# Attention stage of a three-part block: four tiles at a time instead of two, weights moved between ScalarE, VectorE and TensorE

## What is computed

```python
h = x.shape[-1]
proj = x @ W_proj.T
delta, Bs, Cs, residual = jnp.split(proj, 4, axis=-1)
delta = jax.nn.softplus(delta @ W_delta.T + b_delta)
A1 = A[0, 0]
B1 = Bp[0, :, 0]
dA = jnp.exp(delta * A1) * B1
dB = jnp.cumsum(delta * B1, axis=1)
uC = jnp.sum(x * Cs, axis=1, keepdims=True)
Csum = jnp.sum(Cs, axis=1, keepdims=True)
y = dA * uC + dB * Csum
return y + residual * D
...
x = x + 0.5 * _L0_ffn_ref(_layernorm(x, axis=-1), ...)
x = x + _L0_attn_ref(_layernorm(x, axis=-1), ...)
x = x + 0.5 * _L0_ffn_ref(_layernorm(x, axis=-1), ...)
```

## Time and profile before

| | us |
|---|---|
| median of three runs | 1527.41 |
| lowest and highest | 1524.95, 1527.49 |
| the profiled execution, timed from outside | 1527.63 |
| its span, from the first to the last instruction | 1525.8 |
| first and last `x_new` of the attention stage begin at | 649.9, 1096.4 |
| five batches in a row, `a_sums` to `a_sums` | 57.0 each |

### The profile page before, as it was taken

How to read it: one execution, slowest core, us unless ns; L and a number is a source line. 1 busy time by engine, 2 the same in 40 slices (tenths; PEclk the granted TensorE clock), 3 DMA queues, 4 the chain that set the end, 5 groups by cost and what they waited for, 6 DMA issues and landing times. The chain is left out here.

```text
span 1525.8 us, 31260 instructions
## 1 busy us (share of the span) xinstructions
PE 1298.1 (85%) x10212; PEld 1229.3 (81%) x10215; DVE 1239.9 (81%) x3385; ACT 1088.4 (71%) x2343; POOL 675.9 (44%) x778
## 2 busy tenths in 40 slices
PE   5555029999999999799999999987639999999996
PEld 4334019999999999599888888986529999999996
DVE  8999408999999998388999999999837777777775
ACT  6778117777777775589889888886537777777773
POOL 0577752444334444222254554544633344434443
PEclk8877559999999999899999999999859999999999
DMA  9979546766667661921111232111144444444440
GB/s 325 346 271 378 198 160 206 234 223 227 232 207 234 218 212 61 291 72 35 36 62 53 73 102 84 47 60 53 54 144 128 125 148 129 145 147 130 148 130 25
DMA packets 149776, 234.74 MB, mean 154 GB/s; under 512 B 24333, under 2 KB 124390, under 8 KB 147568
## 3 DMA queue, kind: packets, MB, share of 16 engines
q1 hardware_dynamic: 121968, 188.24, 38.2%
q0 software_dynamic: 27648, 44.50, 8.5%
HBM read 128.51 MB, written 136.48 MB: 174 GB/s over the span
## 5 line engine op out<-in xcount | busy, mean ns | idle before, releaser
L1034 PE MATMUL ps<-xs,ws 128*128 128x320 f32 x3072 | 469.6, 311 | 2.2 <-issue 2.2
L1034 PEld LDWEIGHTS ps<-xs,ws 128*128 128x128 f32 x3072 | 454.7, 189 | 8.2 <-issue 8.2
L859 POOL DMA_INDIRECT slots_and_rows<-x x160 | 161.5, 1010 | 238.1 <-DVE x L976 198.5
L859 POOL DMA_INDIRECT out<-x x160 | 157.8, 987 | 236.5 <-DVE x L966 153.8
L1034 PE MATMUL ps<-ws,hs 128*128 128x256 f32 x1920 | 260.6, 289 | 1.3 <-DVE hs L955 1.3
L1034 PEld LDWEIGHTS ps<-ws,hs 128*128 128x128 f32 x1920 | 239.0, 190 | 1.7 <-DVE hs L955 1.7
L898 ACT ACTIVATE x<-x 128x256 f32<-128x256 f32 x320 | 165.0, 594 | 64.8 <-DMA x<-slots_and_rows 49.2
L880 ACT CAST xs<-ps 128x512 fp32r<-128x512 f32 (+1 forms) x192 | 98.3, 513 | 130.4 <-PE ps L1027 130.4
L987 DVE TENSOR_TENSOR hf<-ps,sg 128x320 f32<-128x320 f32 x256 | 124.6, 487 | 81.6 <-ACT sg L919 77.7
L948 DVE TENSOR_TENSOR xs<-ps,xs 128x512 fp32r<-128x512 f32 (+1 forms) x192 | 113.5, 592 | 72.5 <-ACT xs L880 72.5
L373 POOL DMA_INDIRECT slots<-x,slot x128 | 132.9, 1038 | 79.7 <-issue 43.7
(11 more groups left out here) (139 smaller groups left out, 2282.8 us busy)
## 6 DMA issues: line engine op xcount, KB each, us to landing
slots<-blank SPq DMA_DIRECT2D x16, 1310.0 KB
slots_and_rows<-blank SPq DMA_DIRECT2D x32, 655.0 KB, 4.8
x<-slots_and_rows SPq DMA_DIRECT2D x31, 655.0 KB, 3.9
x<-slots SPq DMA_DIRECT2D x31, 655.0 KB, 4.0
x<-slots_and_rows SPq DMA_DIRECT2D x32, 516.0 KB, 8.7
x<-in_x SPq DMA_DIRECT2D x32, 512.0 KB, 8.7
wraw<-in_w_gate SPq DMA_DIRECT2D x64, 256.0 KB
wraw<-in_w_up SPq DMA_DIRECT2D x64, 256.0 KB
```

The source lines that it names most:

```text
L859: nc.gpsimd.indirect_dma_start(out=rows, out_offset=bass.IndirectOffsetOnAxis(ap=factor(e, k, F_ID).bitcast(U32), axis=0), in_=XG[:, e % G ...
L1034: ins = pe.matmul(dst, left(a, k), right(b, k), start=(n == 0), stop=(n == len(terms) - 1))
```

## The change

Softplus, cumulative sum, exponential and mix are done for four tiles (two pairs, called a unit m, 512 rows) at a time. The two PSUM banks now hold one half h of a unit each.

- VectorE: softplus, scan and mix are 128x512 instead of 128x256, half as many. The scan runs in place over CS with a constant 1 as factor. Its two halves stand apart: half 0 in the odd step, behind softplus of the same unit; half 1 at the head of the next step, ahead of the mix. The mix multiplies the exponential by u.
- ScalarE: a new piece, `weight`, makes CS = v*AB + v*b (L1284 of the changed kernel, two instructions of 128x512), at the head of the odd step; `d_a` uses a plain bias. |z+b|, exp, ln and d_a are twice as wide. The logarithm of |u| goes.
- PE: y is turned back by four transposes for a pair, ahead of the residual's products, in place of eight passes against the sign matrices.
- `a_factors` loses the size, sign and diagonal instructions and gains one.
- Buffers: XS has 5 slots, not 3. A pair lies two steps longer in the pipeline (x_new in step n+5, not n+3), and all routing lags move by two steps.

The diff, cut:

```diff
-                TURN, DELTA, PLUS, RES, BACK, LOGIT = 0, 1, 2, 3, 4, 5
+                TURN, DELTA, PLUS, RES, NEW, BACK, LOGIT = 0, 1, 3, 4, 5, 5, 7
...
+                    def weight(m):
+                        a = 2 * m // NC
+                        act.wait_ge(factors.sem, factors.at(a + 1))
+                        act.wait_ge(softplus_done.sem, softplus_done.at(m + 1))
...
                         for h in range(HC):
-                            ins = act.activation(LB[:, a % 2, 1, h:h + 1], LB[:, a % 2, 0, h:h + 1], ACT.Identity,
-                                                 bias=ABD[:, h:h + 1])
-                        ins.then_inc(biased.sem, 1)
...
+                            ins = act.activation(CS[:, m % 2, h, :], AB[:, m % 2, h, :], ACT.Identity,
+                                                 bias=UV[:, a % 2, 2, h:h + 1], scale=UV[:, a % 2, 1, h:h + 1])
+                        ins.then_inc(weighted.sem, 1)
...
                         for h in range(HC):
-                            ins = act.activation(YT[:, n % 2, h, :], AB[:, n % 2, h, :], ACT.Exp,
-                                                 bias=LB[:, a % 2, 1, h:h + 1], scale=A1[:, h:h + 1])
+                            ins = act.activation(YT[:, m % 2, h, :], AB[:, m % 2, h, :], ACT.Exp,
+                                                 bias=ABD[:, h:h + 1], scale=A1[:, h:h + 1])
...
-                        dve.scalar_tensor_tensor(uv[:, 2, :], uv[:, 0, :], -1.0, uv[:, 0, :], ALU.mult, ALU.max)
-                        dve.tensor_scalar(uv[:, 5, :], uv[:, 0, :], 0.0, 2.0, ALU.is_ge, ALU.mult).then_inc(f_links.sem, 1)
...
-                        for h in range(HC):
-                            ins = dve.tensor_scalar(DIAG[:, a % 2, h, :], IDENT, uv[:, 6, h:h + 1], None, ALU.mult)
-                        ins.then_inc(diag.sem, 1)
-                        dve.wait_ge(f_links.sem, f_links.next())
+                        dve.tensor_tensor(uv[:, 2, :], uv[:, 1, :], BD, ALU.mult).then_inc(factors.sem, 1)
...
+                    def scan(m, h):
+                        dve.wait_ge(weighted.sem, weighted.at(m + 1))
+                        dve.wait_ge(scanned.sem, scanned.at(m))
+                        apart(dve)
+                        start = 0.0 if 2 * m % NC == 0 else CS[:, 1 - m % 2, h, QT - 1:QT]
+                        ins = dve.tensor_tensor_scan(CS[:, m % 2, h, :], ONE1[:].to_broadcast([P, QT]), CS[:, m % 2, h, :],
+                                                     start, ALU.mult, ALU.add)
...
-                                ins = pe.matmul(ps[:, BY, j * H + h * P:j * H + (h + 1) * P],
-                                                YT[:, n % 2, h, j * P:(j + 1) * P], DIAG[:, t % 2, h, :],
-                                                start=False, stop=(h == HC - 1), skip_group_check=True)
...
+                                pe.matmul(ps[:, BY, j * H + h * P:j * H + (h + 1) * P],
+                                          YT[:, n // 2 % 2, h, n % 2 * CT + j * P:n % 2 * CT + (j + 1) * P], IDENT,
+                                          start=(j + h == 0), stop=False,
+                                          is_transpose=True, skip_group_check=True)
```

More of the change, by code:

```diff
@@ L1076, in attention @@
                 BZ = (2, 6)
+                QT, XB = 2 * CT, 5
                 stream = stream2
@@ L1249, in x_hi @@
                         act.wait_ge(b_turned.sem, b_turned.at(n + 1))
[L1250 to L1256, removed]
+                        act.wait_ge(residual_done.sem, residual_done.at(n - XB + 1))
@@ L1295, in scalar @@
                         for n in soon(S, TURN):
                             x_hi(n)
+                        for n in at(S, BACK + 1):
+                            tail.act_evac(act, n)
+                        for m in unit(S, PLUS):
+                            d_a(m)
                         for c in parts(S, [p[1] + 1 for p in POST_AT]):
@@ L1420, in vector @@
                             a_sums(a)
-                        for n in soon(S, PLUS):
-                            softplus(n)
+                        for m in unit(S, PLUS + 1):
+                            scan(m, 1)
+                            mix(m)
+                        for n in at(S, NEW):
+                            x_new(n)
+                        for n in at(S, NEW):
+                            dve.wait_ge(x_added.sem, x_added.at(n + 1))
+                            apart(dve)
+                            tail.dve_stats(dve, n)
+                        for m in summed(S):
+                            softplus(m)
                         chosen(S, 5, True)
@@ L1444, in vector @@
                                     tail.dve_moments(dve, n // 2)
+                        for m in unit(S, PLUS):
+                            scan(m, 0)
                         for part in (3, 4, 5, 6, 1, 2, 0):
@@ L1538, in tensor @@
                             sums(a)
+                        for n in at(S, RES):
+                            if n % 2 == 1:
+                                residual(n)
                         for n in soon(S, DELTA):
@@ L1541, in tensor @@
                         counts(S, True)
+                        for n in at(S, RES):
+                            if n % 2 == 0:
+                                residual(n)
                         for n in at(S, LOGIT + 1):
```

173 lines of the change are left out of this document (76 added, 97 removed).

## The result

| | before | after |
|---|---|---|
| median of four runs, us | 1527.41 | 1551.92 |
| lowest and highest | 1524.95, 1527.49 | 1546.23, 1553.4 |
| ratio after to before, 95% interval | | 1.0165 [1.0143, 1.0187] |
| profiled execution, timed from outside | 1527.63 | 1551.43 |
| its span | 1525.8 | 1549.6 |

The change costs 24.5 us; 10.7 were forecast. The direction and the stall were as predicted, the size was not. After the last `x_new` nothing changed: 1525.8 - 1096.4 = 429.4 us remain before, 1549.6 - 1120.1 = 429.5 after.

The account below looks back on a forecast made before the run. VectorE was taken to set the step. Net 0.46 us in 31 double steps gave +14.3; with -6.6, -2.3, +5.0 and +0.3 the sum was +10.7 us, so 1538 us, range 1521 to 1553.

Parts of the forecast that it names:

- Start: Start of the attention stage, up to the first `x_new`: it would come 0.3 us later.
- VectorE, the new wait: VectorE before the scan's half 0: standing 1.68 us for `weight` in place of 0.04, 1.64 us lost a double step.
- ScalarE: ScalarE at 12.15 us a double step: later than VectorE by 0.50 without routing, in some 10 of 31, +5 us.
- PE: Four transposes replace eight sign-matrix passes: 0.3 us a pair saved but hidden; no bound of its own, costs or gives nothing.
- VectorE, width: Wider softplus, scan and mix on VectorE: 1.18 us saved in a double step, 1.05 to 1.30 with the ends.
- The end: Last unit's chain through softplus, weight, scans, mix and residuals, with routing pieces between: taken as 0, 3 us allowed.
- Coupled engines: Rival: ScalarE, PE and VectorE, all near 12 us, obstruct each other; stall 0.5 to 0.6 longer, about 1550; chance 0.22.
- Cheap weighting: Rival: ScalarE's two `weight` instructions cost only a plain copy's 1.07 us; about 1521 us; chance 0.13.
- hidden wait: Rival: `weight` releases the scan before VectorE asks, so only the width counts; about 1482 us; chance 0.03.
- Nothing to measure: Rival: terms cancel within 3 us, 0.2% of the time; chance 0.07 beyond the forecast's own 0.05.

Follow-up runs that it names:

- e6: Changed kernel with each half of `weight` and each half of softplus releasing its waiter separately, no work added or moved; 1519.56 us, ratio 0.9955 to the kernel before.
- e4: Changed kernel with VectorE's copy `a_sums` of the first batch put ahead of the first softplus; 1546.65 us, ratio 1.0136 to the kernel before.
- e7: Changed kernel with the edits of e6 and e4 together; 1519.25 us, ratio 0.9943 to the kernel before.
- e1: Changed kernel with VectorE doing softplus ahead of `x_new` and the statistics in the odd step; 1541.67 us, ratio 1.0097 to the kernel before.
- e3: Changed kernel with the scan reading AB itself, so not waiting for ScalarE, whose weighting goes to an unread buffer; 1523.08 us, ratio 0.9975 to the kernel before.
- e2: Changed kernel with the weighting done on VectorE directly ahead of the scan instead of on ScalarE; 1534.90 us, ratio 1.0052 to the kernel before.

## Why the prediction was off

**Right.** VectorE set the step before, and a change of the stage moves the end one to one (23.7 us at the last `x_new`, 23.8 in the span). The durations: scan 1.265 (1.25 taken), two of `weight` 1.52 (1.50), two of softplus 1.40 and two of the mix 1.41. Pitches of 1.20 and 1.45 for the scans and 1.33 for the mix, where the sum had 1.20, 1.42 and 1.30; only in the first unit of a batch, which the timeline above shows, are the scans' 1.14 and 1.39. a_factors ended 0.87 shorter (0.94). The stall was there 32 times, with 58.6 us in all (52 forecast). ScalarE's double step was put at 12.15 us; the changed kernel has it end to start at 888.52 - 876.34 = 12.18, and so has e6. The run's 1551.9 lies inside the range of 1521 to 1553, close to its upper end, but the sum had 10.7 us of change where 24.5 came. The missing 13.8 us are 7.5 at the start, 3.8 from `x_new` 0 to 56, 1.8 at the end, and 0.7 between the medians and the profiled executions.

**The step that failed most: *Start*, +0.3 against +7.8.** The working followed the chain of `weight` from the factors on and took the factors to be ready about when they were. It did not ask what stands ahead of `a_sums` on VectorE. The first softplus was there before too, but for two tiles, whose ln was done sooner (softplus at 637.30, `a_sums` at 638.09); for four it holds `a_sums` to 641.68. PE's wait for that copy brought the lower clock, which stretched PE's next turns (the four transposes of one take 1.06 us instead of 0.60), and `weight` came to stand behind the rounding that needs them. e4 takes 4.2 of the 7.8 away by exchanging two instructions. Read from the two timelines, each from its first normalisation, 2.3 of these are the copy itself, which begins 18.36 us after that mark and in e4 16.07, and 1.9 lie between the factors and `weight` (3.6 us against 1.7), where PE's slower turns stand. The other 3.6 are, by the timeline alone, the chain through v and the wait for PE, of which the working had 1.5 for `weight`, set against an earlier ready time.

**Two errors that cancel: *VectorE, the new wait* and *ScalarE*.** I took the one hand-over seen inside VectorE (0.18) for two between engines. They are 0.11 to ScalarE and 0.18 back, so the stall is 1.81, not 1.68: over the 28 double steps from `x_new` 0 to 56 the sum had 28 x 0.13 = 3.6 us too little. The ScalarE term of +5 had about as much too much. It was to lengthen the stall beyond 2.0 in ten double steps, four of them in the first batch. The first batch's stalls are 1.80 to 1.85; above that are seven units, at 2.17, 2.09, 2.06, 1.93, 1.90, 1.93 and 1.90, 1.3 us in all beyond 1.81. In a steady batch ScalarE idles 2.67, 0.6 and 3.11 us before three of its `weight`s and is late by 0.09 us, by its own length, only at the one that has no routing work ahead of it on VectorE (888.52). The double step ahead of it took 885.41 - 873.34 = 12.07 us where 12.15 were forecast, but with 0.26 of it a wait of `x_new` for PE. So the forecast of all stalls from `x_new` 0 to 56, 28 x 1.68 + 5.0 = 52.0 us, met the measured 51.9 by luck.

**The 3.8 us short from `x_new` 0 to 56: *PE* and *VectorE, width*.** The sum had 12.9 - 6.6 - 2.3 + 5.0 = +9.0 there, and it is +12.8. These are the largest waits of VectorE in that stretch, before and then after (us in total, times, longest; left out are 1.0 us before and 0.9 after):

```profile
DVE a L1401 <- ACT a L1283: 7.7, 18, 1.2
DVE a L1401 <- DVE a L1392: 6.7, 38, 0.2
DVE a L1381 <- ACT a L1264: 1.5, 2, 1.0
...
```

```profile
DVE blank L1392 <- ACT blank L1284: 51.9, 28, 2.2
DVE a L1402 <- DVE blank L1392: 5.0, 28, 0.2
DVE x L1410 <- PE ps L1522: 3.6, 9, 1.6
DVE a L1351 <- PE ps L1471: 2.9, 2, 2.7
...
```

Without the 1.56 us before the first `x_new`, which belong to the start, these are 17.0 and 62.8 us: +45.8. The rest of the stretch, work end to start, went from 377.9 to 344.9: -33.0. Split the same way, with the hand-over from scan to mix as idle time, the terms were 28 x (1.68 - 0.18) + 5.0 - 2.3 = +44.7 and 28 x (1.18 - 0.18 + 0.04) + 6.6 = -35.7. So 1.1 us are waits: VectorE waited 4.9 us for PE (2.0 before `x_new`, 2.9 before a_sums), which the step *PE* called no bound, and most of that was made up by old waits that went. And 2.7 us are work that the widths and a_factors saved less. Before, in 12 of the 56 pairs a_factors or a routing piece lay behind softplus, and its pitch was then 0.78, not the 0.90 of the earlier trace rows: 1.4 us. The first scans of a batch had a pitch of 1.44 with the hand-over, not 1.57: seven times, 0.9 us. a_factors saved 0.07 less, seven times: 0.5 us.

**The end, 0 against +2.** The last seven pairs took 3.4 us more, where three and a half units of 0.46 give 1.6. e6 and e7 still take 53.4 and 53.6 against 51.55 before. In the changed kernel VectorE stands idle there before pieces of the next stage's normalisation and routing (1.2 us before L348, 1.0 before L508, 1.0 before L474), and before the change it did so for none of them. (Before, `x_new` waited there 2.7 us in two waits for L1519, the product with the sign matrices, of which the step *PE* says that it never ended a wait of VectorE's.) No run isolates these waits, so the cause stays open; 3 us were allowed for it in the text.

**The rivals.** *Coupled engines* forecast 1550, close to the 1552 measured, but by luck, not by its reason: its 0.55 us longer stall in the routed double steps is not in the trace (1.81 in all three). The mechanism came out only in e1. *Cheap weighting* is refuted by the duration (1.52), *hidden wait* by 58.6 us of idle time. Nor are the 45 us of gain that *hidden wait* had for the widths to be had by taking the stall away: with all of it gone (e3) the kernel is 3.7 us faster than before, the 6.4 us of its later start included, since VectorE then waits for ScalarE's rounding. *Nothing to measure* is refuted by the interval of the ratio, 1.0143 to 1.0187.

The step that the prediction lacked altogether is the choice of granularity: it took for given that the scan waits for both halves of `weight`, and `weight` for both of softplus. Both signals stand behind the loop over the halves, as the code in the change shows, and moving them into it was worth 1551.9 - 1519.6 = 32 us.

## What to carry to other kernels

When work is widened, the release gets coarser with it unless each half keeps its own signal. The price of a round trip to another engine is then one whole loop there and two hand-overs; released by halves it is one piece and two hand-overs, less what the sender still has to do. So look first at what is signalled after the last instruction of a loop that could be signalled after the first. Doing the small thing oneself, even on the fuller engine, was better than the coarse round trip (e2, 17 us below the changed kernel), but the round trip released by halves was better still (e6, 15 us below e2). And price the start of a pipeline on its own: list for each engine what stands ahead of the first instruction that others wait for. Last, split a forecast total into its terms before calling it right: here a stall of 52 us was met because two errors of nearly 4 us cancelled.

## What the runs showed of the hardware

- TensorE's granted clock fell to 0.50 (1.2 GHz) after PE had stood 2.92 us, and to 0.50 to 0.72 over the same 3 us in the five other runs with that wait; in e4 and e7, with 0.65 us as the wait for the same copy, it stayed at 1.00.
- A hand-over from VectorE to ScalarE took 0.11 us, one from ScalarE to VectorE 0.18, one from VectorE to itself 0.18.
- A scan of 128x512 took VectorE 1.22 us in the first unit of each batch, where its start is a constant, and 1.28 in all others, where it is a column of a buffer.
- A multiplication and addition with two pointers took VectorE 557 ns for 128x512, where a multiplication with a single pointer took 479; the same as the first on ScalarE took 808.
- Between executions the first stage alone varied by 2.8 us (the first normalisation of the attention stage at 621.22 to 624.02), so a term of the start is measured from a mark behind it.
